# A vision tower on one core: the diffuser's reference tiles, weight splitting and leftover steps put in other places, and its masks made in two parts

## The reference, cut to what matters

```python
h = tokens(x) @ W + b
# masks: cosine of a small encoder's output with that of the references
cos = einsum(enc(xm), enc(ref)) / norms;  m = 0.5 + 0.5 * tanh(25 * ((mean_r(cos) + 1) / 2 - 0.5))
z = xm * m
for _ in range(3):                 # STEPS
    q, v = heads(z @ qv_w);  a = q k_r^T * scale;  o = mean_r((a a^T) v)
    z = layernorm(scramble(o) @ proj_w + proj_b)
d = concat(m * z + (1 - m) * xm, ref)
h = layernorm(h + d)
t = h + attention(layernorm(h))    # softmax attention, 12 heads
h = layernorm(h + t + moe(layernorm(t)))   # 8 experts, top 2, gelu
```

## Time and profile before

| | us |
|---|---|
| median of 3 runs | 439.36 (437.77 to 446.16) |
| profiled execution | 436.05 |
| its span, first to last instruction | 434.2 |
| PE busy | 372.4 (86% of the span) |
| DVE, ACT, POOL busy | 239.0, 204.6, 216.2 |
| token stage and masks, to PE's first diffuser transpose | 0 to 54.5 |
| diffuser steps 0 to 23 on PE | 54.5 to 162.8 |
| attention and rest of the diffuser | 167.3 to about 290 |
| experts and end | to 434.2 |

### The profile page before, as it was taken

The page is one execution under the profiler, slowest core; times in us unless marked ns, Lnnn a source line. Parts: engine busy times, 40 slices in busy tenths (PEclk is TensorE's granted clock), DMA queues, the critical chain, the costliest instruction groups (busy, mean ns, idle before and its releaser), DMA issues.

```text
span 434.2 us, 11094 instructions
## 1 busy us (share of the span) xinstructions
PE 372.4 (86%) x3714; PEld 317.1 (73%) x3714; DVE 239.0 (55%) x713; ACT 204.6 (47%) x518; POOL 216.2 (50%) x359
## 2 busy tenths in 40 slices
PE   4999588999999974698888999962599999999963
PEld 3888465767676743587888899952499989899963
DVE  2101333445454553256677776656388888888623
ACT  1222156677776753436456555520445544554103
POOL 1001154476667677215477675345156676666414
PEclk9999879999999995579899999965599999999967
DMA  8998507666566521100000001003777766765052
GB/s 240 387 384 288 176 0 167 162 137 153 119 138 160 131 31 17 23 2 1 2 17 18 11 17 31 19 16 120 255 273 258 262 220 249 253 250 203 7 176 68
DMA packets 59558, 59.08 MB, mean 136 GB/s; under 512 B 36939, under 2 KB 46197, under 8 KB 58736
## 3 DMA queue, kind: packets, MB, share of 16 engines
q1 hardware_dynamic: 57248, 54.81, 40.9%
q0 software_dynamic: 2256, 3.57, 2.6%
HBM read 25.11 MB, written 14.33 MB: 91 GB/s over the span
## 4 chain that ended last, share of the span: by engine, by line
PE 76%; DVE 6%; ACT 5%; POOL 5%; issue 4%; DMA 2%; SPq 1%; ACTq 0%; POOLq 0%; DVEq 0%
PE bank L409 37%; PE wide L409 32%; PE bank L414 4%; PE bank L697 1%; ACT xT L905 1%; DMA xT<-in_xT 1%; ACT xTs L794 1%; PE bank L610 1%; POOL rstd L1261 1%; DMA xT<-y_dram 1%; POOL w2l L1293 1%; ACT hT L794 0%; DMA y_dram<-ysb,ydst 0%; DMA xT<-srt_dram 0%; POOL y_dram L1333 0%
## 5 line engine op out<-in xcount | busy, mean ns | idle before, releaser
L1260 POOL TENSOR_SCALAR veps<-mv 108x1 f32<-108x1 f32 x46 | 10.4, 226 | 69.9 <-DVE mv L975 68.4
L1333 POOL DMA_INDIRECT y_dram<-ysb,ydst x25 | 25.9, 1037 | 35.4 <-DVE ydst L1214 27.6
L409 PE MATMUL wide<-w2h,xs 128*128 x300 | 39.1, 246 | 0.0
L768 ACT ACTIVATE xT<-bank 108x192 f32<-108x192 f32 (+3 forms) x57 | 21.0, 369 | 34.1 <-PE bank L409 17.6
L409 PE MATMUL wide<-w2l,xs 128*128 x150 | 36.9, 246 | 0.0
L1208 DVE TENSOR_TENSOR xs<-xT,xs 128x384 bf16<-128x384 f32 x50 | 35.6, 712 | 1.7
L409 PE MATMUL bank<-wqv,xTs 128*108 128x384 f32 x96 | 36.4, 503 | 0.1
L794 ACT ACTIVATE xT<-bank,gains 96x128 f32<-96x128 f32 x50 | 20.0, 448 | 32.3 <-PE bank L697 32.3
L1206 DVE CAST xs<-xT 128x384 f16<-128x384 f32 x50 | 29.0, 580 | 9.9 <-ACT xT L940 8.9
L409 PE MATMUL wide<-xT 64*108 64x36 f32 (+2 forms) x368 | 31.5, 280 | 1.7 <-DVE chosen L1101 0.9
L409 PEld LDWEIGHTS wide<-xT 64*108 64x108 f32 (+1 forms) x368 | 29.2, 182 | 3.9 <-issue 3.3
(11 more groups left out here) (241 smaller groups left out, 1052.6 us busy)
## 6 DMA issues: line engine op xcount, KB each, us to landing
srt_dram<-row SPq DMA_DIRECT2D x8, 800.2 KB, 15.2
xT<-in_xT SPq DMA_DIRECT2D x11, 324.0 KB
tokw<-w1h SPq DMA_DIRECT2D x9, 384.0 KB
e1T<-w1l SPq DMA_DIRECT2D x9, 384.0 KB
xT<-in_w SPq DMA_DIRECT2D x8, 384.0 KB, 3.2
hT<-in_w SPq DMA_DIRECT2D x8, 384.0 KB, 3.3
vecs<-w1h SPq DMA_DIRECT2D x8, 384.0 KB
wqv<-w1l SPq DMA_DIRECT2D x8, 384.0 KB
```

The costliest lines, as they stand in the source:

```text
L409: return nc.tensor.matmul(o, l, r, start=start, stop=stop)
L768: return nc.scalar.activation(o, i, ACT.Copy)
L1260: link(G.tensor_scalar(ve, var, EPS, None, ALU.add))
L1333: G.indirect_dma_start(y_dram, bass.IndirectOffsetOnAxis(ydst[:, q:q + 1], 0), ysb[:, q % YB], None, bounds_check=2 * NTOK - 1, oob_is_err ...
```

## The change

- The products of the reference rows with `sel` move from `s == 9` to `s == 8` on PE; the encoder output of tiles 0 to 2 (`EARLY_T = 3`) is taken at `s == 9` and their masks are made inside the token stage. The masks of tiles 3 to 7 are made during step 0. PE's token loop is one turn shorter, and its last encoder product stands behind `to_features(0)`.
- The reference tiles' `combine`, double root and `rows_of` move from steps 21 to 23 to steps 11 to 13 (`REFS_AT = NT`); `rows_of` stands in steps 14 and 15.
- `turn_of(q)`: two pieces in each of steps 0 to 4, then one a step in steps 5 to 18. SP loads the next piece at the head of its iteration, ahead of the store of the result; it waits there for the split of the same step.
- DVE's buffer setup moves to step 20 (`prepare`), `to_columns(0)` and `columns(0)` into step 23, and the table of the exponential is loaded in step 0 by a one-column activation.
- In attention turns 0 to 4 the leftover of the diffuser no longer stands first: its parts are spread behind the wide products.

```diff
-            if 0 <= i - NI + AHEAD < NT:
-                numbered.append(("first", i - NI + AHEAD))
+        def begun(i):
+            return i - REFS_AT if i < NI else i - NI + AHEAD
...
         def turn_of(q):
-            return max(0, q - 1)
+            return q // 2 if q < 10 else q - 5
...
@@ sync @@
             for i in range(NI + 1):
+                for q in (q for q in range(4, PIECES) if turn_of(q - 4) == i):
+                    sp.wait_ge(S["low_ready"], q - 3)
+                    piece(q)
                 if i < NI:
                     sp.wait_ge(S["o_ready"], i + 1)
...
-                for q in (q for q in range(4, PIECES) if turn_of(q - 4) == i):
-                    sp.wait_ge(S["low_ready"], q - 3)
-                    piece(q)
...
@@ tensor, token stage @@
-            for s in range(NT + 3):
+            for s in range(NT + 2):
...
+                    if s - 3 == NR + EARLY_T - 1:
+                        last.then_inc(S["exa_psum"], 1)
...
             to_features(0)
+            t = TILES[NT - 1]
+            pe.wait_ge(S["e1_ready"], NT)
+            mm(bank[5][0:T, (t - EARLY_T) * E2:(t - EARLY_T + 1) * E2], e1T[:, t * T:(t + 1) * T], fc2[:]).then_inc(S["ex_psum"], 1)
...
@@ tensor, attention @@
             for i in range(NT + 4):
-                if i < 5:
-                    step(NI + i)
...
+                if i < 5:
+                    turn_result(NI - 5 + i, NI)
+                if i == 0:
+                    products_r(NI - 1)
...
+                if i == 0:
+                    products_o(NI - 1)
+                    values(i)
...
+                if i < 5:
+                    projection(NI - 5 + i)
...
@@ scalar @@
+                if s == NT:
+                    squash(0)
-            nc.scalar.activation(mask[:, 0:1], rowm[:, 0:1], ACT.Tanh)
-            act.wait_ge(S["cos_ready"], 1)
-            nc.scalar.activation(th[:], cosm[:], ACT.Tanh, scale=12.5).then_inc(S["th_ready"], 1)
...
             for i in range(NI):
                 step(i)
-                if i >= NI - 2:
-                    rows_of(i - NI + 2)
+                if i == 0:
+                    squash(1)
+                    nc.scalar.activation(vv[:, 1, 0:1], rowm[:, 0:1], ACT.Exp)
+                if i - REFS_AT - AHEAD in range(2):
+                    rows_of(i - REFS_AT - AHEAD)
...
@@ vector @@
+                if s == 9:
+                    dve.wait_ge(S["rb_psum"], 1)
+                    link(V.tensor_copy(rb[:], bank[5][0:T, 128:128 + E2]))
+                    dve.wait_ge(S["exa_psum"], 1)
+                    nets(0, EARLY_T, bank[7])
                 if s == 10:
+                    closeness(0, EARLY_T)
...
+                    masks(0, 0, EARLY_T)
...
+            dve.wait_ge(S["ex_psum"], 1)
+            nets(EARLY_T, MT, bank[5])
             for i in range(NI):
                 step(i)
-                if i >= NI - AHEAD:
-                    combine(i - NI + AHEAD)
-            dve.wait_ge(S["low_ready"], PIECES)
+                if i == 0:
+                    closeness(EARLY_T, MT)
+                    masks(1, EARLY_T, MT)
+                if begun(i) in range(AHEAD):
+                    combine(begun(i))
+                if i == turn_of(PIECES - 1) + 2:
+                    prepare()
...
```

More of the change, by code:

```diff
@@ L38 @@
 NR = NT - MT + 1
+EARLY_T = 3
 P = 128
@@ L465, in _ @@
                     last.then_inc(S["k_psum"], 1)
+                if s == 8:
+                    pe.wait_ge(S["exn_ready"], 1)
+                    for i in range(NR):
+                        rows = T if i < NR - 1 else LAST
+                        last = mm(bank[5][0:T, 128:128 + E2], sel[0:rows, int(i > 0), :], ex[0:rows, MT - 1 + i, :], i == 0, i == NR - 1)
+                    last.then_inc(S["rb_psum"], 1)
                 if s == 9:
@@ L532, in step @@
[L532 to L541, removed]
@@ L563, in to_columns @@
+                for k in range(2):
+                    last = mm(bank[2][0:T, 0:2 * C], xTs[:, i % 2, k, :], wqv[:, k, :], k == 0, k == 1)
+                last.then_inc(S["qv_psum"], 1)
+                if q >= 0:
+                    products_r(q)
+                if p >= 0:
+                    projection(p)
+                if q >= 0:
+                    products_o(q)
             def to_columns(a):
@@ L589, in features, with values @@
                 return last
+            def values(i):
+                pe.wait_ge(S["ak_ready"], i + 1)
+                for k in range(2):
+                    last = mm(bank[2][0:T, 2 * T:2 * T + C], x1T[:, i % 2, k, :], wvo[:, 0, k, :], k == 0, k == 1)
+                last.then_inc(S["av_psum"], 1)
             for i in range(NT + 4):
-                if i < 5:
-                    step(NI + i)
                 if i < NT:
@@ L649, in _ @@
                     last.then_inc(S["s_psum"], 1)
-                    for k in range(2):
-                        last = mm(bank[2][0:T, 2 * T:2 * T + C], x1T[:, i % 2, k, :], wvo[:, 0, k, :], k == 0, k == 1)
-                    last.then_inc(S["av_psum"], 1)
+                    if i >= 1:
+                        values(i)
                 if 1 <= i <= NT:
@@ L773, in _, with squash @@
             halves2 = bank[0][0:HF, 2 * T:4 * T].rearrange("p (f t) -> p f t", f=2)
-            for s in range(NT + 3):
+            def squash(n):
+                span = slice(0, EARLY_T) if n == 0 else slice(EARLY_T, MT)
+                act.wait_ge(S["cos_ready"], n + 1)
+                nc.scalar.activation(th[:, span], cosm[:, span], ACT.Tanh, scale=12.5).then_inc(S["th_ready"], 1)
+            for s in range(NT + 2):
                 if 0 <= s - 2 < NT:
```

306 lines of the change are left out of this document (168 added, 138 removed).

## The result

Four runs of the changed kernel gave a median of 420.08 us (417.67 to 424.15), beside 438.56 us (437.20 to 446.16) for the kernel before on the same chip: a ratio of 0.9583 with a 95% interval of 0.9519 to 0.9647. The forecast was 421.0. The profiled execution took 417.67 us with a span of 415.8 (forecast 418 and 416.2).

What follows compares the result with a forecast made beforehand. PE, 86% busy, was taken as the bound where its clock is full. Terms -22.4 - 5.4 + 1.4 + 6.9 + 1.5 = -18.0 took the span from 434.2 to 416.2 us, the median to 421; 8-in-10 range 411 to 431.

Steps and rivals of the forecast that it cites:

- The join: From wqv of step 22 to attention turn 5: 76.5 us fall to 54.1, a gain of 22.4; bounds 16 to 25.
- Rival D: At the join: the attention waits for another thing than the pieces; given no chance of its own.
- Masks: Before the diffuser's first steps: masks in two parts remove PE's idle time and half clock, -5.4 us; bounds -6.7 and -2.
- what is late next: Steps 0 and 1: the second mask part, with qp, vm and the next wqv behind the table load, costs +1.3 us.
- Two pieces a step: Steps 0 to 4: ACT at times waits for a piece, 0.5 us in three of five steps, +1.4; bounds 0 and +5.
- the rest: 0: SP's later stores in steps 12 to 14, DVE's setup at step 20 and the experts' queues: 0 us.
- rival C: SP's new order: a late split delays the store, PE waits for oc; slower, about 449 us; chance 0.03.
- Reference tiles: Steps 11 to 13: double roots beside splits overload POOL by 7.6 us, and PE loses +6.9; lower bound 0.
- Rival A: Steps 11 to 13: POOL's overload is swallowed by slack; about 412.5 us; chance 0.19.
- Cold clock: Around POOL's overload: PE idle a third of the time may lower its clock, +1.5 us; bounds 0 and +5.
- Table load: Step 0: the exponential's table load on ACT, priced at the trace's 1.28 us, not the skill's about 2.66.
- Rival B: Steps 0 to 4: POOL and the ring of four stages bound, giving most gain back; milder form about 430 us; chance 0.15.

Runs made afterwards that it cites:

- Head: Changed kernel with what is left of the diffuser at the head of attention turns 0 to 4 again; 430.75 us, ratio 0.9926.
- split_old: Changed kernel with the weight pieces split one a step up to step 22 as before, buffer setup in step 23; 426.9 us, ratio 0.9795.
- mask_one: Changed kernel with the masks of all eight tiles made in one part behind the token stage; 421.1 us, ratio 0.9681.
- sp_order: Changed kernel with SP storing the result first and loading the next weight piece behind it; 429.98 us, ratio 0.9633.
- refs19: Changed kernel with the reference tiles' combine and double root in steps 19 to 21 instead of 11 to 13; 415.74 us, ratio 0.9526.
- after_again: The changed kernel itself, run and profiled again (the second profile); 422.42 us, ratio 0.9644.
- exp_early: Changed kernel with the exponential's table load ahead of qp of step 0; 416.38 us, ratio 0.9325.
- head14: Changed kernel with the diffuser's leftover at the head of attention turns 1 to 4, turn 0 as changed; 431.51 us, ratio 0.9819.
- shift: Changed kernel with every weight piece one step later, none in step 0, buffer setup in step 21; 421.09 us, ratio 0.9618.

## Why the prediction was right

**The sum.** Forecast -18.0 for the span, measured -18.4; every row of the table above lies within 2.5 us of its term. Part of that closeness is luck: the terms' errors (+1.4, -2.4, -1.4 and +1.6) cancel, and the second profile gives -12.3. What the four runs say, 420.08 against 421, doesn't hang on that one profile.

**The join (-22.4; measured -24.8).** Right in size, and by its own steps: turns of 7.6, 8.4, 9.1, 9.0 and 9.3 us against 8.0 and four of 9.5. What failed is the reason given. "It holds the 10 us of waiting" names the splits as the cause, and I gave the new order in the turns nothing of its own beyond the round figure of 9.5 a turn. Head shows that of 24.8 us the placing holds 15.7: with every wait for a piece gone, the leftover in front still cost a wait of 2.06 us and the clock for 16. The late pieces alone cost 6.1 (split_old), so the two parts don't quite add up to 24.8: behind the waits of either the clock was down. Rival D, another wait at the join, is excluded by the largest wait there, 0.36 us.

**Masks (-5.4).** Too large for a usual run: against mask_one, step 5 is 5.2 us earlier in the first profile and 1.5 in the second, and the ratios give 2 to 4, not told from none. What was not seen is the split beside the cosine product. "POOL does 2 x 1.64" counted POOL's time and not what DVE loses beside it. The part that was mis-sized is "what is late next": a chain of small operations was priced as if DVE ran alone, and PE's wait of 2.44 us for `rm`, with the half clock behind it, was not in the 1.3.

**Two pieces a step (+1.4; +1.75 between steps 2 and 5).** The size held. The nearest pair is mask_one and the kernel before, both with the masks in one part: 21.05 against 19.95 us for steps 0 to 5, so +1.1, with the table load in it. The profiles with the masks in two parts can't settle it: 22.5 us in split_old, 22.6 to 25.9 with two pieces a step and the load in its place, the long ones with the clock down. The way was as forecast too, ACT waiting for a piece's load (2.30 us in step 4), but in one step and not in three: that spacing was 5.62 us, before 4.10. But "the rest: 0" took SP's order as a by-product and looked at it only for harm (rival C). It carries the two pieces: without it this part costs about 10 us more (36.0 against 25.9). Rival C itself fell: in the overload SP's store held nobody up, PE's printed waits there are for `xT` L1154 and ACT's `xs`, none for `oc`, and sp_order shows the same spacings (5.94, 7.24, 6.82) from step 13 to 16.

**Reference tiles (+6.9; +6.84 between steps 13 and 16).** Held, and by its steps: the three spacings lost 1.6, 2.9 and 2.4 us. The 1.64 and 0.58 us of slack were the right ones to set against 7.6 us of excess. Rival A, that slack swallows it, is excluded by the trace and by refs19.

**Cold clock (+1.5).** In the first profile one `wqv` took 2.50 us and nothing was lost: mask_one, whose clock stayed at 1.00, takes the same 82.04 us from step 5 to 22. In after_again two spacings were 8.29 and 4.92 instead of 6.83 and 4.44, 1.9 us more. So between 0 and 1.9. I weighed there a rule of the Trainium skill (TensorE: Matmul & The Clock Gate, Part 1): the clock follows how busy the array has been recently. That half rate would be reached "for certain" was my own reading of it, and the runs don't bear it out. With the same spacings the clock fell for part of a step in the first profile (at 124 us), was at 0.56 and 0.58 from 126 to 138 us in after_again, and stayed at 1.00 in mask_one and head.

**Table load.** The trace and exp_early show 1.28 us, by the earlier trace rows and again at 52.27. The Trainium skill (ScalarE: Activation LUTs, "What ACT_TABLE_LOAD costs") gives about 2.66 with the drain; no wait ahead of the load was seen in either place, so here the measured 1.28 stands.

**Rival B** (early part gives most back) did not hold in the changed kernel, but sp_order is what it looks like: the ring of stages as the bound of steps 0 to 4.

Open: whether the falls of the clock in the turns of head and head14 come from the printed waits alone or also from many shorter gaps. No run separates them; a wait of 0.92 us ahead of turn 1 left the clock at 1.00 in the changed kernel, and with one as long head14's was at 0.50 some 1 us later.

## What to carry to other kernels

Before a helper engine gets two more pieces of work per step, follow its loads back to the queue that issues them: a load that stands behind a result's store turns the two into one ring. Work left over from a stage is worth more behind wide products than in front of a turn, also where no long wait is seen: a wait of 2 us in front was followed by some 16 us at half clock. And one profile of each kernel is not enough to price a change of a few us: compare the stretch that the edit touches, in more than one profile. Last, an overload that was forecast from slack against excess can be avoided by placing the work where the same engine has finished its other list.

## What the runs showed that was not expected

- A DVE operation with two SBUF inputs lasted until POOL's splits ended: 0.15 us alone and 1.92 or 1.93 beside two of them (seven profiles), 0.36 alone and 1.33 and 2.06 for `finish`. POOL's splits kept their 1.64 and 2.37 us in the rows printed here. `vm`, which reads a PSUM bank (matmul results) and one SBUF input, stayed at 0.75 or 0.76. The Trainium skill (SBUF — State Buffer, "Terms") describes the pair of ports that DVE and POOL share as exclusive for an instruction's length; the traces agree, and two splits back to back did not let this operation in between.
- The same kernel's profiled span was 415.8 and 421.9 us: 3.3 us of it in steps 0 to 5, with a cosine product that started 3.0 or 1.3 us into the splits, and 1.9 in steps 15 to 17, where the clock fell.
- Behind turn 5, where the edits change next to nothing, the 14 profiles take from 203.3 us (head) to 212.5 (shift). That is as much as most of these edits are worth.
